# Cross-network tower kernel: three partial sums in column pairs merged by one tensor_reduce, and the top layer's first matmuls moved ahead of the last G

## The reference

```python
e = stack([tbl_m[ids[:, m]] for m in range(40)], axis=1)     # 512 x 40 x 16
x = e
for k in (k0, k1, k2):                                       # 128 x 40 x 40, 128 x 128 x 40 twice
    x = einsum('bhd,bmd,ohm->bod', x, e, k)
    outputs.append(sum(x, axis=-1))
z = concatenate(outputs, axis=1)                             # 512 x 384
h = concatenate([z, dense_ctx], axis=1)                      # 512 x 400
h = maximum(h @ W_top1 + b_top1, 0)
h = maximum(h @ W_top2 + b_top2, 0)
y = h @ W_top3
```

## Time and profile before

| | |
|---|---|
| median of 3 runs | 753.32 us (752.2 to 756.63) |
| the profiled execution, its own time | 758.32 us |
| its span | 756.4 us |
| busy in the span: PE, DVE, ACT, POOL | 677.2 (90%), 674.5 (89%), 523.3 (69%), 523.3 (69%) us |
| granted TensorE clock, mean | 0.98 of full |
| DMA | 43.08 MB, mean 57 GB/s |

### The profile page before, as it was taken

The page is one execution under the profiler, slowest core; times in us unless marked ns, Lnnn a source line. Parts: engine busy times, 40 slices in busy tenths (PEclk is TensorE's granted clock), DMA queues, the critical chain, the costliest instruction groups (busy, mean ns, idle before and its releaser), DMA issues.

```text
span 756.4 us, 12855 instructions
## 1 busy us (share of the span) xinstructions
PE 677.2 (90%) x2558; PEld 468.6 (62%) x2558; DVE 674.5 (89%) x1542; ACT 523.3 (69%) x1753; POOL 523.3 (69%) x443
## 2 busy tenths in 40 slices
PE   0388999999988989899889999998989999998998
PEld 0255767676665757576656667575757666773483
DVE  2559999999989999999899999999999999989291
ACT  2247777677776868777767868586877777887293
POOL 6549786878869697978698787879687874572000
PEclk9989999999999999999999999999999999997699
DMA  6451211212121312121211313030212111100000
GB/s 200 130 194 43 75 42 42 75 35 72 21 83 28 84 32 73 43 73 43 61 43 23 93 19 91 22 87 28 75 42 75 43 49 65 46 1 29 1 0 1
DMA packets 56679, 43.08 MB, mean 57 GB/s; under 512 B 37007, under 2 KB 40335, under 8 KB 56352
## 3 DMA queue, kind: packets, MB, share of 16 engines
q1 hardware_dynamic: 51488, 41.08, 18.1%
q0 software_dynamic: 5120, 1.32, 1.8%
HBM read 40.41 MB, written 1.97 MB: 56 GB/s over the span
## 4 chain that ended last, share of the span: by engine, by line
PE 44%; DVE 29%; issue 17%; DMA 3%; POOL 2%; ACT 2%; DVEq 2%; SPq 1%; ACTq 0%; POOLq 0%
DVE chain L540 15%; PE Y L628 11%; PE Y L630 10%; PE Y L629 10%; DVE chain L503 8%; PE X L595 4%; DVE pairs L468 3%; DVE pairs_lo L475 2%; DMA pairs<-scratch 2%; POOL x0g L315 1%; ACT scaled L423 1%; PE GB L602 1%; PE X L656 1%; PE X L654 1%; PE X L655 1%
## 5 line engine op out<-in xcount | busy, mean ns | idle before, releaser
L423 ACT ACTIVATE scaled<-Y,xtok 128x128 f32<-128x128 f32 x1536 | 421.8, 381 | 128.8 <-PE Y L630 108.8
L628 PE MATMUL Y<-k1lo,x1hi 128*128 128x512 f32 x640 | 292.0, 456 | 21.0 <-DVE chain L540 19.5
L630 PE MATMUL Y<-k1hi,x1lo 128*128 128x512 f32 x640 | 254.1, 397 | 0.0
L629 PE MATMUL Y<-k1hi,x1hi 128*128 128x512 f32 x640 | 253.2, 396 | 0.0
L315 POOL DMA_INDIRECT x0g<-in_table,rows_now x160 | 204.8, 1280 | 42.1 <-issue 36.9
L540 DVE SCALAR_TENSOR_TENSOR chain<-Y,xtok,chain 128x128 f32<-128x128 f32 x768 | 211.4, 337 | 3.9 <-PE Y L630 3.8
L356 POOL TENSOR_TENSOR fold<-fold,scaled 128x512 f32<-128x512 f32 x128 | 174.3, 1362 | 22.0 <-ACT scaled L423 11.5
L628 PEld LDWEIGHTS Y<-k1lo,x1hi 128*128 128x128 f32 x640 | 120.8, 189 | 91.6 <-DVE chain L540 52.6
L356 POOL TENSOR_TENSOR fold<-scaled 128x512 f32<-128x512 f32 x64 | 90.3, 1411 | 87.8 <-ACT scaled L423 65.3
L629 PEld LDWEIGHTS Y<-k1hi,x1hi 128*128 128x128 f32 x640 | 121.3, 190 | 38.6 <-issue 14.4
L630 PEld LDWEIGHTS Y<-k1hi,x1lo 128*128 128x128 f32 x640 | 120.8, 189 | 29.5
(11 more groups left out here) (77 smaller groups left out, 464.6 us busy)
## 6 DMA issues: line engine op xcount, KB each, us to landing
pairs<-scratch SPq DMA_DIRECT2D x112, 240.0 KB
A<-scratch SPq DMA_DIRECT2D x16, 240.0 KB
k1raw<-in_k SPq DMA_DIRECT2D x1, 2560.0 KB, 9.7
x0g<-in_table,rows_now POOLq DMA_INDIRECT x160, 2.8
k2s<-in_k SPq DMA_DIRECT2D x1, 2560.0 KB, 10.1
scratch<-x0g SPq DMA_DIRECT2D x96, 20.0 KB, 1.7
pairs<-in_w SPq DMA_DIRECT2D x3, 256.0 KB, 2.9
w2s<-in_w SPq DMA_DIRECT2D x1, 512.0 KB, 3.9
```

The lines of the kernel that those rows point to most:

```text
L423: ins = nc.scalar.activation(scaled[:, rank(c) - 1, i * O:(i + 1) * O], Y[(NCH * tile + c) % YB][:, i * O:(i + 1) * O], ACT.Copy, scale=xt ...
L628: nc.tensor.matmul(y, hi[:, tok], k1lo[:, cols], start=True, stop=False)
L629: nc.tensor.matmul(y, hi[:, tok], k1hi[:, cols], start=False, stop=False)
L630: nc.tensor.matmul(y, lo[:, tok], k1hi[:, cols], start=False, stop=True).then_inc(s_y, 1)
```

## The change

The three sums of a tile now lie in one tensor `parts` (128 x 3 x 512, twice): part 0 is the chain, part 1 the fold, part 2 ACT's sixth chunk, which ACT writes there directly instead of into `scaled`. In each 512-column part the four 128-column blocks no longer lie one after another: `block_of` puts blocks 0 and 1 side by side, column by column (o of block 0, o of block 1, next o), and blocks 2 and 3 likewise. So ACT and DVE now write, and DVE reads, with a step of two elements; POOL's additions stay 512 wide and contiguous. One `tensor_reduce` over 1536 elements per partition, whose innermost step takes the two neighbours of a pair, makes x2 of 128 columns, in place of the four additions. It stands behind chunk 2 (`MERGE_AT = 2`). It waits for the chain, all of ACT's chunks and all folds of the tile at once. ACT's sixth chunk now waits for the merge of two tiles before (its buffer is double) instead of the first merge step of the tile before. At the end, PE waits per output block for the one bank that it overwrites, and does the z0 and context matmuls of the first two blocks ahead of the last `make_G`, and the other two behind it.

```diff
-EXTRA = NA - 2 - FOLDS
-MERGE = EXTRA + 3
+DIRECT = NA - 2 - FOLDS
+PARTS = 2 + DIRECT
...
-MERGE_AT = (0, 3, 3, 3)
+MERGE_AT = 2
...
-        scaled = sb("scaled", [P, NA, BANK])
-        fold = [sb(f"fold{i}", [P, BANK]) for i in range(2)]
-        chain = [sb(f"chain{i}", [P, BANK]) for i in range(2)]
+        scaled = sb("scaled", [P, NA - DIRECT, BANK])
+
+        parts = [sb(f"parts{i}", [P, PARTS, BANK]) for i in range(2)]
+        chain, fold = ([parts[i][:, k, :] for i in range(2)] for k in range(2))
...
+        def block_of(chunk, i):
+
+            return chunk.rearrange("p (k o t) -> p k t o", k=MB // 2, t=2)[:, i // 2, i % 2, :]
...
                             else:
-                                act.wait_ge(s_merge, MERGE * (T + 1) + rank(c) - NA + EXTRA)
+                                act.wait_ge(s_merge, T + 1)
...
+                            to = (scaled[:, rank(c) - 1, :] if rank(c) <= NA - DIRECT else
+                                  parts[tile % 2][:, 2 + rank(c) - 1 - NA + DIRECT, :])
                             for i in range(MB):
                                 m = c * MB + i
                                 ins = nc.scalar.activation(
-                                    scaled[:, rank(c) - 1, i * O:(i + 1) * O],
+                                    block_of(to, i),
...
-            def merge(T, par, k):
-
-                sums = chain[par]
-                if k == 0:
-                    dve.wait_ge(s_chain, STT * (T + 2))
-                else:
-                    dve.wait_ge(s_merge, MERGE * (T + 2) + k)
-                if k < EXTRA:
-                    dve.wait_ge(s_yA, NA * (T + 2) - EXTRA + k + 1)
-                    a, b, to = sums[:, :], scaled[:, NA - EXTRA + k, :], sums[:, :]
-                elif k == EXTRA:
-                    dve.wait_ge(s_fold, FOLDS * (T + 2))
-                    a, b, to = sums[:, :], fold[par][:, :], sums[:, :]
-                else:
-                    n = BANK >> (k - EXTRA)
-                    a, b = sums[:, 0:n], sums[:, n:2 * n]
-                    to = sums[:, 0:n] if k < MERGE - 1 else x2[par][:, :]
-                nc.vector.tensor_tensor(to, a, b, ALU.add).then_inc(s_merge, 1)
...
+            def merge(T, par):
+
+                dve.wait_ge(s_chain, STT * (T + 2))
+                dve.wait_ge(s_yA, NA * (T + 2))
+                dve.wait_ge(s_fold, FOLDS * (T + 2))
+                nc.vector.tensor_reduce(x2[par][:, :], parts[par][:, :, :].rearrange(
+                    "p k (j o t) -> p o (k j) t", o=O, t=2), AX.XY, ALU.add).then_inc(s_merge, 1)
...
                                 nc.vector.scalar_tensor_tensor(
-                                    out=chain[tile % 2][:, i * O:(i + 1) * O], in0=Y[(NCH * tile + c) % YB][:, i * O:(i + 1) * O],
+                                    out=block_of(chain[tile % 2], i), in0=Y[(NCH * tile + c) % YB][:, i * O:(i + 1) * O],
                                     scalar=xtok[slot % 2][:, j, m:m + 1],
-                                    in1=chain[tile % 2][:, i * O:(i + 1) * O] if n >= MB else scaled[:, 0, i * O:(i + 1) * O],
+                                    in1=block_of(chain[tile % 2] if n >= MB else scaled[:, 0, :], i),
...
             over_groups(pe, body)
-            make_G(NTILES - 1, (NTILES - 1) % 2)
-

             pe.wait_ge(s_mlp, 8 * 16)
-            pe.wait_ge(s_chain, STT * (NTILES + 1))
-            pe.wait_ge(s_yA, NA * (NTILES + 1))
             pe.wait_ge(s_x1free, NG)
             for i in range(H1 // P):
+
+                c = NCH - YB + (i - (NCH * NTILES - YB)) % YB
+                if OWNER[c] == "A":
+                    pe.wait_ge(s_yA, NA * NTILES + rank(c))
+                else:
+                    pe.wait_ge(s_chain, STT * NTILES + MB * rank(c))
                 o = slice(i * P, (i + 1) * P)
                 nc.tensor.matmul(Y[i][:, :], w1s[0][:, o], z0[:, :], start=True, stop=False)
                 nc.tensor.matmul(Y[i][:, :], w1cs[:, o], ctxs[:, :], start=False, stop=False)
+                if i == 1:
+                    make_G(NTILES - 1, (NTILES - 1) % 2)
```

More of the change, by code:

```diff
@@ L184, in build @@
         w1cs, ctxs = A3[0][0:CTX, :], A3[1][0:CTX, :]
-        z2, w2s = pairs[3], over("fold0", "w2s", [P, H1 // P, H2])
+        z2, w2s = pairs[3], over("parts0", "w2s", [P, H1 // P, H2])
         h1 = scaled[:, 0:H1 // P, :]
@@ L189, in build @@
         Ghi = x1hi + pairs_hi[0:2]
-        Glo = x1lo + [pairs_hi[2], over("chain0", "Glo3", [P, B], f32r)]
+        Glo = x1lo + [pairs_hi[2], over("parts1", "Glo3", [P, B], f32r)]
         h2, ys = G[:, 0:2, 0:B], G[0:1, 2, 0:B]
@@ L203, in build @@
         s_gather, s_rows = [sem(f"gathered{i}") for i in range(2)], sem("rows_ready")
-        s_k1hi, s_k1lo, s_w0sum, s_dzero, s_dones, s_szero = [sem(n) for n in (
-            "k1hi_ready", "k1lo_ready", "w0_summed", "diag_zeroed", "diag_ones", "scaled_zeroed")]
+        s_k1hi, s_k1lo, s_w0sum, s_dzero, s_dones = [sem(n) for n in (
+            "k1hi_ready", "k1lo_ready", "w0_summed", "diag_zeroed", "diag_ones")]
         s_trans = sem("tokens_transposed")
@@ L219, in build @@
         s_fold = sem("pool_folds")
-        s_merge = sem("tile_sums_merged")
+        s_merge = sem("tile_parts_summed")
         s_diag, s_G, s_Gout = sem("diag_ready"), sem("g_filled"), sem("g_copied")
@@ L298, in _ @@
             sp.dma_start(ctxs[:, :], ctxT).then_inc(s_mlp, 16)
-            sp.wait_ge(s_merge, MERGE * (NTILES + 2))
+            sp.wait_ge(s_merge, NTILES + 2)
             sp.dma_start(w2s[:, :, :], w2.rearrange("(c p) n -> p c n", p=P)).then_inc(s_w2, 16)
@@ L329, in _ @@
             pool.wait_ge(s_dones, 2)
-            nc.gpsimd.memset(fold[1][:, :], 0.0).then_inc(s_fold, FOLDS)
+            nc.gpsimd.memset(credit[:, 5:6], 0.0).then_inc(s_fold, FOLDS)
             nc.gpsimd.memset(credit[:, 0:1], 0.0).then_inc(s_G, 1)
@@ L350, in body @@
                     sums = fold[tile % 2]
-                    pool.wait_ge(s_merge, MERGE * T + 1)
-                    for a in range(2, NA - EXTRA):
+                    pool.wait_ge(s_merge, T + 1)
+                    for a in range(2, NA - DIRECT):
                         pool.wait_ge(s_yA, NA * (T + 1) + a + 1)
@@ L484, in prep @@
                                             ALU.add).then_inc(s_x1free, 1)
[L486 to L507 removed]
+            def merge(T, par):
[4 more added lines that the diff above has]
+                    "p k (j o t) -> p o (k j) t", o=O, t=2), AX.XY, ALU.add).then_inc(s_merge, 1)
+            nc.vector.memset(parts[1][:, :, :], 0.0).then_inc(s_chain, STT)
+            nc.vector.memset(credit[:, 4:5], 0.0).then_inc(s_merge, 1)
             dve.wait_ge(s_w0, 32)
@@ L546, in body @@
                             prep(step, u, slot)
-                        for k in range(MERGE):
-                            if c == MERGE_AT[k]:
-                                merge(T - 1, (tile - 1) % 2, k)
+                        if c == MERGE_AT:
+                            merge(T - 1, (tile - 1) % 2)
             over_groups(dve, body)
-            for k in range(MERGE):
-                merge(NTILES - 1, (NTILES - 1) % 2, k)
-            dve.wait_ge(s_merge, MERGE * (NTILES + 2))
+            merge(NTILES - 1, (NTILES - 1) % 2)
+            dve.wait_ge(s_merge, NTILES + 2)
             for c in range(NCH):
@@ L598, in make_G @@
             def make_G(T, buf):
-                pe.wait_ge(s_merge, MERGE * (T + 3))
+                pe.wait_ge(s_merge, T + 3)
                 pe.wait_ge(s_diag, T + 2)
@@ L661, in _ @@
             pe.wait_ge(s_w2, 16)
+            pe.wait_ge(s_chain, STT * (NTILES + 1))
+            pe.wait_ge(s_yA, NA * (NTILES + 1))
             for k in range(H1 // P):
```

9 lines of the change are left out of this document (3 added, 6 removed).

## The result

The changed kernel takes 702.73 us (median of 4 runs, 701.21 to 703.93), the one before on the same chip 754.98 (752.2 to 757.7): a ratio of 0.9307, 95% interval 0.9263 to 0.9351. The gain is 52 us by the medians and 55 by the two profiled executions (758.32 to 703.25; the one before was 3 us above its median); 61 were forecast; 702.7 lies in the stated range, 10.7 above the 692 that was predicted.

The account below looks back on a forecast made before the run. DVE was taken to bound groups that carry preparation, busy 39.77 of 40.30 us. 47 us from the loop and 14 from the end made 61; 758.3 became 697, less 5.0 for the median: 692 us, range about 677 to 713.

Parts of the forecast that it names:

- the floor: PE's time for a group that carries preparation, if PE does the same work: 36.2 us against 40.32 before.
- Part 1: Merge on DVE: one reduce of 1.7 us replaces four additions of 3.75 per tile; DVE's group becomes 31.6 us.
- Part 2: Column pairs: DVE's products and ACT's scalings step by two elements; taken to cost nothing, at most 9.8 us per group.
- rival 4: Strided products on DVE make the change slower: 763 us, chance 0.09.
- turning point: Strided products on DVE: at 0.14 us more per product, the end's 14 us were said to be eaten up.
- Part 3: Waits in the loop: engine coupling costs 1.0 us above PE's floor, groups take 37.2 us, fifteen groups win 47 us.
- It fits, barely: POOL in a group: 32.47 busy and 2.3 us of issue gaps make 34.8 of the coming 37 us.
- the returns of the loop: Longer group distances where the loop returns, 44.12 us against 40.32: all three were expected to stay.
- Part 4: End of the kernel: z0 and context matmuls fill PE's pause, layer 2 starts at 698.2 instead of 712.5: 14 us.
- Rival 1: PE's clock does not stay up at the end: 6.6 us more, 699 us, chance 0.15.
- Rival 2: The reduce on DVE is slow, 3.4 us: 718 us; chance 0.17, including a milder stride cost.
- Rival 3: POOL or the five-bank handshake, not DVE, keeps groups at 40.3 us; only the end is won: 739 us, chance 0.04.

Follow-up runs that it names:

- later products: Changed kernel with the first pair product at position 8 of a group instead of 6, the others 2 later, layer 0 by 1: 702.75 us.
- early gathers: Changed kernel with GATHER_TILES 3 to 2, so POOL issues a group's ten gathers in its first two tiles: 695.03 us.
- the two runs: Kernel before with only the new order at the end: 746.32 us; changed kernel with the order of the end put back: 715.79 us.
- old end: Changed kernel with the end of before, the last G first, then z0 and context matmuls: 715.79 us.
- plain layout: Changed kernel with the four blocks of a part one after another, the reduce taking 12 elements 512 bytes apart: 718.65 us.
- sorted end: Changed kernel with the end's matmuls as four z0, the last G, four context: 704.40 us; with early gathers as well 697.14 us.
- all three: Changed kernel with early gathers, sorted end and later products together: 706.89 us.

## Why the prediction was right, and where it was off

**The sum.** Of the 10.7 us between 692 and 702.7, 5.5 are the loop (47 forecast, 41.5 measured), 0.5 the end, and some 4.5 a step that had no cause behind it: the profiled execution of before lay 5.0 above the median of its runs, and the forecast took these 5.0 off the changed kernel too. Its profiled execution lay 0.5 above the median (703.25, 702.73). A reason that fits the mean clocks above, and was not tested, is that the runs of before differ by how long the clock stays at 0.50 behind the pause, and that this went with the pause.

**The bound of before** was read rightly: with 15.0 us of merges replaced by 7.0, groups fell by 2.4 us, and the floor that was worked out from the rows, 36.2, was met at 36.18 once nine of ten gathers were left out.

**Part 1.** The reduce was put at 1.7 us and takes 1.74, without spread. Right.

**Part 2.** Products unchanged, rightly; rival 4 falls, for this layout. Its mechanism is real and lies one step further on: at 16 bytes a product costs 0.10 us more. Its turning point was added up wrongly: 31.6 + 0.5 + 64 x 0.14 is 41.1 and not 41.2, and at 0.14 us that takes back 11 of the end's 14 us.

**Part 3 is the step that was off.** "I let the coupling of the engines cost 1.0 us above PE's floor" was a choice without a row; it measured 1.7, and the run with one gather gives all of it to the gathers. "It fits, barely" had named POOL, but counted only its busy time and issue gaps. Also, "part of it is time that it loses to DVE's additions" looked at one side: POOL's gathers did get shorter (1280 to 1066 ns), but with the additions gone DVE's pair products grew from 865 to 1080 ns; that is 1.5 us per group that DVE's forecast load of 31.6 does not hold. That the collision moved from the additions to them fits the rows and was not shown by a run. The wait for the reloaded rows, 9.6 us in all before and 21.4 after, was not in the forecast; taking it away by later products won nothing. In the other direction, that the returns of the loop "stay" was wrong: they fell from 3.8 to 1.3 us, PE's pause behind them from 2.3 to 0.6. The prediction counts three; two of the fourteen distances are long. The early gathers brought them back to 5.0, with pauses of 2.9 us and the clock at 0.50 behind them. What makes the pauses was not tried.

Fifteen groups at 37.2 with returns as before would have been 47 us; the loop gave 41.5 (39.5 between the marks and 2.0 around them), the merge's part by run 42.1.

**Part 4.** 14 us forecast, 13.55 in the traces, 11.6 and 13.2 by the two runs. The 1.3 us by which alternating passes were dearer than 0.43 were not foreseen; the merge came when expected. The size holds for an execution in which the clock stays low as long as in that profile; in the profile of the old end the pause cost 5.0 us. So what the end is worth differs from run to run, by the clock of the kernel before, and the agreement to half a microsecond is partly luck.

**Rival 1** did not come in the changed kernel: its clock stayed at 1.00 to layer 2. But its mechanism is real. In the profile of the plain layout the clock fell at the same end with no gap on PE, which cost 1.7 us (13.7 from the first z0 matmul to layer 2 against 12.0), and twice it fell in the sorted end, which cost 3.35 us each time (14.19 against 10.84). The rival had priced it at 6.6.

**Rival 2** did not come, but a slow reduce was built by hand with the plain layout: 2.9 us, and then 718.65 us, where 3.4 us had been priced at 718. That near hit is luck. By the rival's own sum 2.9 us give a group of 31.6 + 4.8 + 0.5 = 36.9, under the 37.2 forecast, and so no loss; measured, groups came to 38.6.

**Rival 3** came in a small part: by the run with one gather it is POOL's gathers that hold a group now, at 37.9 and not at 40.3.

## What to carry to other kernels

When three sums of an engine must become one, lay them so that the reader takes pairs of neighbours and the writers step by no more than 8 bytes; then a single reduce replaces a chain of additions at 1.1 ns per element (1743 for 1536), and it is not stretched beside a busy GpSimd. Once the bound engine is relieved, work out the next engine's floor from its own rows, and distrust any sum of busy times for the engine between: a trial that leaves its work out tells in one run how much of the rest is its fault. Fill a pause of PE with work that is ready rather than shorten it: what the pause costs afterwards in clock varies from run to run, by 8.6 us between two profiles here. Read the granted clock of the filled stretch in more than one run, though. It can fall there too, and with eight 16-row passes in a row it fell in two profiles of four.

## What the runs showed of the hardware

- DVE and ACT, fp32, 128 elements: a step of two elements (8 bytes), on output and input of DVE and on output of ACT, cost next to nothing (340 ns against 339 in the plain layout and 336 before on DVE, 387 against 382 on ACT); a step of four (16 bytes) cost 103 ns, 0.80 ns per element, on both. A reduce whose every element lies 512 bytes from the last cost 0.76 ns per element more than one in pairs.
- A two-operand addition of 128 columns from SBUF had a median of 1269 ns over the kernel before and took 291 to 294 in its last group. Where it took 1.27 us (614.40), a fold of POOL had begun before it (613.99, 1.54 us); a reduce of 1536 elements in its place stayed within 22 ns over the whole run.
- After a pause of 3.05 us the TensorE clock stood at 0.50 for 3 to 4 us in one execution, and after one of 3.46 us for 20 us in another, under the same order of matmuls and with PE busy throughout.
- In three profiles the clock fell to 0.50 while PE was busy 97 to 100% of each microsecond: for 3.4 us in passes alternating between 128 and 16 rows (plain layout), and for 6.7 us in eight passes on 16 rows (early gathers with sorted end, all three). It stayed at 1.00 in the seven other profiles with the alternating end and in the two others with the sorted one. The Trainium skill (TensorE: Matmul & The Clock Gate, Part 1) has the clock set by how busy PE has been recently; with PE's busy share as the measure, neither these falls nor the 20 us at 0.50 agree with it.
- Full-precision passes that alternate between operands of 128 and of 16 rows took 0.53 us each at full clock, sorted ones 0.43 to 0.46.
